# Edge stage of a four-layer graph network: 40 early and 80 direct chunks instead of 48 and 72, in turns of D D E D D E with four direct row buffers

## The reference

```python
def _L3_gnn_ref(x, edge_index, We1, be1, We2, be2, Wn1, bn1, Wn2, bn2):
    def _mlp(h, W1, b1, W2, b2):
        return jax.nn.relu(h @ W1 + b1) @ W2 + b2
    src = edge_index[0]
    dst = edge_index[1]
    e_in = jnp.concatenate([x[src], x[dst]], axis=-1)
    edge_new = _mlp(e_in, We1, be1, We2, be2)
    agg = jax.ops.segment_sum(edge_new, dst, num_segments=x.shape[0])
    mesh_new = _mlp(jnp.concatenate([x, agg], axis=-1), Wn1, bn1, Wn2, bn2)
    return x + mesh_new
...
x = _layernorm(x + _L0_gnn_ref(x, ...))   # three GRU rounds over segment sums
x = _layernorm(x + _L1_gnn_ref(x, ...))   # hypergraph convolution
x = _layernorm(x + _L2_gnn_ref(x, ...))   # attention over the edges
x = _layernorm(x + _L3_gnn_ref(x, ...))
```

## Time and profile before

| | us |
|---|---|
| three timed executions | 4739.2, 4741.78, 4747.91 |
| their median | 4741.78 |
| span of the profiled execution | 7303.0 |
| busy in that span: PE, PEld, DVE | 4076.2, 3354.5, 3381.7 |
| busy in that span: ACT, POOL | 2340.3, 2658.9 |

### The profile page before, as it was taken

One profiled execution on the slowest core, in us unless ns is written; L12 is line 12 of the kernel. 1 busy time (PEld: TensorE's weight loads), 2 busy tenths in 40 slices (PEclk: granted clock), 3 DMA queues, 4 the chain that ended last, 5 costly groups with the idle time before them and its releaser, 6 DMA issues. The chain is left out here.

```text
span 7303.0 us, 82736 instructions
## 1 busy us (share of the span) xinstructions
PE 4076.2 (56%) x24237; PEld 3354.5 (46%) x24238; DVE 3381.7 (46%) x7886; ACT 2340.3 (32%) x3120; POOL 2658.9 (36%) x2706
## 2 busy tenths in 40 slices
PE   4332641019981111117989798988672197666655
PEld 2111420007761101106778586858571197665644
DVE  4222540358970000106788776456451076555545
ACT  0000010005640000004555455557461075444433
POOL 4555157730017777770000000000427601444463
PEclk7665865559995555558999898989785598888777
DMA  9400000009970000116658287843444343444432
GB/s 376 155 0 0 0 2 0 0 23 334 368 250 0 0 0 0 28 25 222 232 189 293 96 293 214 296 162 95 132 125 124 97 139 98 132 132 130 130 95 67
DMA packets 364823, 923.20 MB, mean 126 GB/s; under 512 B 114026, under 2 KB 138716, under 8 KB 364531
## 3 DMA queue, kind: packets, MB, share of 16 engines
q1 hardware_dynamic: 214722, 650.09, 26.9%
q10 hardware_dynamic: 58609, 180.13, 6.4%
q0 software_dynamic: 91200, 89.42, 5.2%
HBM read 705.69 MB, written 213.71 MB: 126 GB/s over the span
## 5 line engine op out<-in xcount | busy, mean ns | idle before, releaser
L1741 POOL DMA_INDIRECT edges_halves<-local,gather_idx x832 | 854.9, 1027 | 791.7 <-SPq L372 505.4
L1680 POOL DMA_INDIRECT adj_t<-cell_val,cell_at x832 | 828.6, 996 | 465.2 <-issue 369.9
L862 PE MATMUL ps<-tiles_r,stage_r 128*128 128x512 f32 x2028 | 811.6, 400 | 158.2 <-issue 132.0
L1134 POOL DMA_INDIRECT big<-table,gather_idx x576 | 548.4, 952 | 832.3 <-DVE stage L1284 376.3
L869 PE MATMUL ps<-stage,big 128*128 128x130 f32 x4046 | 520.1, 284 | 370.3 <-issue 354.7
L1134 POOL DMA_INDIRECT x_fm<-table,gather_idx x384 | 370.2, 964 | 959.8 <-DMA table<-cell_at 689.7
L869 PEld LDWEIGHTS ps<-stage,big 128*128 128x128 f32 x4046 | 497.9, 199 | 388.5 <-issue 384.6
L2059 PE MATMUL ps<-big,ident_h 128*128 128x104 bf16 (+1 forms) x2880 | 359.7, 256 | 460.4 <-issue 459.7
L1253 PE MATMUL ps<-big,stage 128*128 x1920 | 356.2, 342 | 352.7 <-issue 189.3
L1319 PE MATMUL ps<-ident,big 128*128 128x128 f32 x260 | 73.3, 377 | 817.2 <-issue 768.2
L2442 DVE TENSOR_TENSOR big<-ps,stage 128x1248 bf16<-128x1248 f32 x192 | 270.7, 1451 | 519.5 <-remote 385.1
(11 more groups left out here) (482 smaller groups left out, 9007.8 us busy)
## 6 DMA issues: line engine op xcount, KB each, us to landing
onehot<-adj_t SPq DMA_DIRECT2D x332, 512.0 KB
big<-adj_t SPq DMA_DIRECT2D x332, 512.0 KB
onehot<-adj_s SPq DMA_DIRECT2D x170, 512.0 KB
adj_t<-rows ACTq DMA_DIRECT2D x13, 6656.0 KB
adj_s<-big ACTq DMA_DIRECT2D x157, 512.0 KB, 5.3
stage<-local_rows SPq DMA_DIRECT2D x120, 512.0 KB
big<-adj_s SPq DMA_DIRECT2D x84, 512.0 KB
x_fm<-adj_s SPq DMA_DIRECT2D x84, 512.0 KB
```

The costliest lines, as they stand in the source:

```text
L862: nc.tensor.matmul(psum_fm(p, n)[:, 0:cut], upper_rows[:, k, :], tile[:, 0:cut], start=k == 0, stop=False, skip_group_check=True)
L1134: return nc.gpsimd.indirect_dma_start(out, None, table[0:N, :], bass.IndirectOffsetOnAxis(gather_idx[:, t:t + 1], 0))
L1680: nc.gpsimd.indirect_dma_start(out, bass.IndirectOffsetOnAxis(cells[:, c:c + 1], 0), cell_val[:, c:c + 1], None).then_inc(S(name), 16)
L1741: nc.gpsimd.indirect_dma_start(edges_halves, bass.IndirectOffsetOnAxis(slot_at[:, at:at + 1], 0), slot_val[:, at:at + 1], None).then_inc(h ...
```

## The change

40 chunks are early instead of 48 and 80 direct instead of 72. A turn is D D E D D E, so 20 turns hold all 120 chunks and `SPARE` becomes 0. There are four direct row buffers and two early ones, the same six in all. Turn 0 and turn 19 are unrolled, turns 1 to 18 rolled. SP issues its early loads at two places of a turn instead of three, each behind a wait for the add of the chunk three back instead of four. The lines behind the constants keep their numbers less two (POOL) or three (the other engines).

```diff
-HOT = 3
+HOT = 4
...
-EARLY = 48
+EARLY = 40
 EARLY_PAIRS = EARLY // 2
 DIRECT = CHUNKS - EARLY
-TURN = "DEDEDE"
+TURN = "DDEDDE"
 LOOPS = EARLY // TURN.count("E")
 PER_TURN = TURN.count("D")
 SPARE = DIRECT - PER_TURN * LOOPS
...
             with eng.Fori(GROUPS, LOOPS - 1) as i:
                 turn(i, True)
             turn(LOOPS - 1, True)
-            for x in range(1, SPARE + 1):
-                body(Spot(0, 0, x))
...
                 if spot.h == 5 and not (spot.known and spot.i == LOOPS - 1):
-                    early(EARLY_SLOTS * (spot.i + 1), 0, spot.u - 4)
-                if spot.h in (1, 3) and not (spot.known and spot.i == 0):
-                    slot = (spot.h + 1) // 2
-                    early(EARLY_SLOTS * spot.i + slot, slot, spot.u - 4)
+                    early(EARLY_SLOTS * (spot.i + 1), 0, spot.u - 3)
+                if spot.h == 2 and not (spot.known and spot.i == 0):
+                    early(EARLY_SLOTS * spot.i + 1, 1, spot.u - 3)
```

## The result

The changed kernel takes 4613.39 us (median of four, 4601.46 to 4614.86) against 4742.0 before: a ratio of 0.9718, interval 0.9701 to 0.9734. That is 128.6 us less.

What follows compares the result with a forecast made beforehand. POOL's gathers, 10.06 us a chunk against the engines' 6.53, were taken to bound the 24 chunks behind the loop. Tail -64, rolled code +27, start -12, loop 0: -49 us, 4693, range 4660 to 4752.

Steps and rivals of the forecast that it cites:

- tail: 24 unrolled direct chunks behind the edge loop: their wait for POOL's gathers goes, -64 us.
- rival 4: Tail behind the loop: all of the recorded 127 us is real, giving -112 us, 4630; chance 0.06.
- start: Start of the edge stage: fewer early pairs let the first direct rows land on time, -12 us (-18 to 0).
- 24 chunks rolled: Edge stage: 24 chunks move from unrolled code into four more rolled turns, +27 us (+11 to +47).
- loop: Rolled edge loop: POOL's four direct chunks a turn, 40.2 us, fit turns of 41.8 to 46 us; 0 change.
- rival 1: Gathers: the 0.30 us gaps may belong to recording, so timed runs are not POOL-bound; +14, 4756 us; chance 0.11.
- Rival 2: Edge loop: POOL becomes its bound with slower gathers; at 1.8 us a gather +44, 4786 us; chance 0.03.
- rival 5: Rolled loop: rolled code is free, four more turns cost 0.4 us instead of 27; 4666 us; chance 0.07.
- about 1000 us were left for the edge stage: Edge stage: other stages add up to about 3740 us of 4742, leaving about 1000, good to some tens.
- POOL's indirect DMAs hold the other engines back while a profile is taken: Profile before: back-to-back scatters hold other engines' instructions; the same 364 matmuls take 918 us beside scatters, 95 without.

Runs made afterwards that it cites:

- -63 alone: Kernel before, the 24 chunks behind the loop gathering only their first four tiles (96 gathers left out): 4680.08 us, 0.9861.
- unstretched record: Kernel before run once more with no edit, for a profile that the recording does not stretch: 4743.21 us, span 4741.5.
- -64 alone: Kernel before, the last four early pairs not gathered (64 gathers left out), their stores still issued: 4679.26 us, 0.9864.
- +72 put back: Changed kernel, POOL gathering and storing the last four early pairs twice, 24 pairs of early work as before: 4684.92 us, 0.9877.

## Why the prediction was wrong: the start

| term | predicted | measured |
|---|---|---|
| tail | -64 (-127 in rival 4) | -63 alone; 61.8 us of DVE's waits in the unstretched record |
| start | -12 (0 to -18) | -64 alone (7.8 us of the wait left); +72 put back; a wait of 76.9 us gone |
| 24 chunks rolled | +27 (+11 to +47) | +9 to +11 |
| loop | 0 | 0: POOL still waits for DVE, 24.9 us in all |
| sum | -49 | -64 - 63 + 10 = -117 by the single runs, -77 - 62 + 10 = -129 by the records' waits; measured -128.6 |

That the second sum meets the measured time within 1 us is in part chance: the spans of the two unstretched records differ by 141.8 us (4741.5 and 4599.7), 7.9 of it ahead of the last table store (3693.35 and 3685.41).

**The tail** came out as worked. That the gathers' 0.30 us gaps hold in timed runs too (against rival 1) is settled by the same runs: without the gaps, the forecast's own count left 12.8 us, and 63 were measured. Rival 2 did not come up.

**The start is the step that failed.** It said "Then come the first direct rows, 10.06 and 1.8. They land at 391 to 399 where DVE wants them at about 382: 9 to 17 late." The lateness of the early work was there in its own numbers: 379 to 386 us after the 6th table store for the last early store, 319 for the last table store. Three things went wrong with it.

- *The consumer.* I asked only who waits for the *gathered rows* and took the first matmul of the loop as the due time; ScalarE's copy at the head of the stage waits for the same stores, to reuse `x_fm`, and behind it stand the rest of the copies, the q rows, SP's loads and the first matmul. Its due time is about 10 us after the last table store (3703.57 - 3693.35 in the unstretched record), not 60.9. With it the forecast's own numbers give 379 to 386, and 3.9 from the end of the store to its landing (3776.58 to 3780.49), against 329: 54 to 61 late, near the 64 and 72 that the runs gave.
- *The due time.* From the last table store to the first edge matmul it is 60.9 us in the stretched record, but 33.8 in the changed kernel's (3685.41 to 3719.20). With 33.8 DVE wants the rows at about 355 (319, 33.8 and the forecast's 2), and its 391 to 399 are 36 to 44 us late. So the stretched distance hid 27 us even for the consumer that I looked at.
- *The length of the early work.* In the unstretched record the last early store starts 405 us after the sixth table store (3775.82 - 3370.89), not 379 to 386. Its 404.9 and 4.7 to the landing, against 322.5 for the last table store and 10.2 to the eleventh copy, are the 76.9 us of the wait.

It is no surprise of the chip but a wait in the program that the list of waits on `early_stored` shows in one look; it carries no time in the stretched record, because there the early work was done 296 us ahead, and I took "no row" for "no wait".

**Rolled code was oversized.** The turn of 46.0 us at clock 0.80 was taken as the typical one. The loop's windows in the two unstretched records, before and after (columns as in the earlier trace rows):

```profile
3806.00:4470.20 664.20, 477.63 (x3145) 427.64 (x3146) 446.38 (x1049) 338.88 (x400) 366.22 (x386) 0.89 0.49 151
```

```profile
3758.00:4500.00 742.00, 511.84 (x3456) 458.68 (x3456) 497.88 (x1171) 371.45 (x439) 548.47 (x578) 0.91 0.49 151
```

One turn before:

```profile
3971.24 1.29 DVE L1284 TENSOR_TENSOR stage<-ps,big 128x512 f32<-128x512 f32 x2 [1.27 <-issue]
...
4013.07 1.29 DVE L1284 TENSOR_TENSOR stage<-ps,big 128x512 f32<-128x512 f32 x2 [1.27 <-issue]
```

Turns are 41.8 us long in both (3926.11 to 3967.95 after), as six chunks at clock 0.99 would be (6 x 6.97), although the granted clock of the loop is 0.89 and 0.91: some matmuls run at 1.2 GHz, and these turns are no longer for it. A rolled chunk costs 0.36 (unrolled kernel) to 41.8/6 - 6.53 = 0.44 us more than an unrolled one, the lower end of the forecast. That rolled code is free (rival 5) falls too, since unrolling 18 turns gained 38 to 42 us. The Trainium skill, "Advanced Engine Details and Errata", section "Control Flow Timing", gives about 108 ns for a compare-and-branch. By that figure one a turn would make an estimated 1.9 us of those 38 to 42. The longer idle time before an add stands in every chunk of a turn, not once a turn. The order on DVE has register instructions within each chunk; that these are the cost is likely, but no run tries them apart from the branch.

Rival 4's 4630 was the nearest number, but by a mechanism that did not hold, so its nearness is luck: the tail was worth 63 us, not the 127 of the stretched record. The estimate that about 1000 us were left for the edge stage, 30 more than the forecast could fill, was the one sign in the working that something of that size was missing, and it was used only against rival 1.

## What to carry to other kernels

Before a transfer's end is called hidden, list every wait on its semaphore and on the buffer that it reads, with the due time of each; a buffer that is reused can have an earlier due time than the data. Where a profile is much longer than the timed runs, it can also reverse the order in which two engines finish, so a wait that shows no idle time in it is not yet a wait that costs nothing. Work that one engine can do only at its own pace is best spread under the others: 24 chunks at the end at POOL's pace cost 63 us; spread over the turns they cost the 9 to 11 us of rolled code, and DVE waits for no rows.

## What the runs showed that was not expected

- The record of one and the same program spanned 7303.0 us at clock 0.754 in one execution and 4741.5 at 0.905 in another, with the timed runs at 4742 in both cases. PE's idle time for "issue" beside POOL's scatters came with the first alone: in the second, with the same scatters, line 1319 has 31.8 us of it in all. So the prediction's reading, that POOL's indirect DMAs hold the other engines back while a profile is taken, does not hold of recording as such. What makes a record stretch was not tried.
- In the changed kernel a gather took 0.954 us on the mean in the edge stage and 1.071 beside the attention pass (the two group lines of the page above). An early pair took 22.9 us there (first gather at 3224.98, last store at 3683.54, twenty pairs), where the forecast had 376.5 / 17 = 22.1.
- Unrolling the changed kernel's edge stage gained 42 us, 0.9% of the whole. That longer code would cost as much as it saves was not seen.
